# Widening the reciprocals of the softmax sums on VectorE, and the steps of a 16-group pipeline in a new order

## The reference, cut to what matters

```
x = x + attn_mlp(_layernorm(x))   # sliding window of 128, 16 heads of 16; then MLP 256 -> 1024 -> 256
x = x + rwkv_ffn(_layernorm(x))   # r = sigmoid(xr W_r); k = relu(xk W_k)^2; r * (k W_v)
x = x + mamba(_layernorm(x))      # ED 512, N 16: h = exp(delta A) h + delta B x;  y = h C + D x
x = x + expert(_layernorm(x))     # one of 8 experts for each batch, picked by the mean over its tokens
# in the attention:
scores = jnp.where(valid, scores, -jnp.inf)          # 128 queries x 256 keys for each head
attn = jax.nn.softmax(scores, axis=-1)
out = jnp.einsum('bhcqk,bhckd->bhcqd', attn, vcat)
```

## Time and profile before

| | us |
|---|---|
| median of 3 runs | 3138.97 (3136.85 to 3139.93) |
| profiled execution | 3140.19 |
| its span, first to last instruction | 3138.4 |
| mean granted TensorE clock in it | 0.946 of 2.4 GHz |
| one period of the pipeline, from 589.70 to 2591.42 us / 11 | 181.97 |

### The profile page before, as it was taken

The page is one execution under the profiler, slowest core; times in us unless marked ns, Lnnn a source line. Parts: engine busy times, 40 slices in busy tenths (PEclk is TensorE's granted clock), DMA queues, the critical chain, the costliest instruction groups (busy, mean ns, idle before and its releaser), DMA issues. The chain is left out here.

```text
span 3138.4 us, 54529 instructions
## 1 busy us (share of the span) xinstructions
PE 2770.5 (88%) x17328; PEld 1768.4 (56%) x17328; DVE 2498.8 (80%) x5626; ACT 2402.0 (77%) x5299; POOL 2657.6 (85%) x1596
## 2 busy tenths in 40 slices
PE   5888887899999999999899999989999998988667
PEld 3554454465665656566565656656565665654336
DVE  3257979888787978888787887978788897889880
ACT  6587879788787978888797887879798787865532
POOL 1108999999999999999999999999999999999880
PEclk9899999999999999999999999999999999998778
DMA  3004353446445454644546364445546455365541
GB/s 85 14 36 151 122 186 121 164 142 219 135 149 174 154 193 134 222 144 145 173 150 204 124 224 141 153 154 157 201 130 222 143 162 172 125 216 163 191 145 42
DMA packets 285965, 477.31 MB, mean 152 GB/s; under 512 B 38450, under 2 KB 93362, under 8 KB 285682
## 3 DMA queue, kind: packets, MB, share of 16 engines
q1 hardware_dynamic: 285682, 473.83, 46.0%
HBM read 388.79 MB, written 84.93 MB: 151 GB/s over the span
## 5 line engine op out<-in xcount | busy, mean ns | idle before, releaser
L1826 POOL TENSOR_TENSOR h_rows<-u_rows,b_rows 128x1024 f32<-128x1024 f32 x512 | 1201.6, 2370 | 39.3 <-PE bank L968 29.9
L1836 POOL TENSOR_TENSOR h_rows<-h_rows,c_rows 128x1024 f32<-128x1024 f32 x486 | 1145.4, 2369 | 43.6 <-DVE state L1606 30.2
L1280 ACT ACTIVATE bank<-d_rows,a_rep 128x512 f32<-128x512 f32 x1024 | 673.3, 687 | 236.6 <-DMA d_rows<-delta_dram 55.8
L1599 DVE TENSOR_TENSOR_SCAN h_rows<-bank,h_rows 128x512 f32<-128x512 f32 x492 | 586.1, 1211 | 37.0 <-ACT bank L1280 34.2
L1599 DVE TENSOR_TENSOR_SCAN h_rows<-bank,state,h_rows 128x512 f32<-128x512 f32 x480 | 590.1, 1266 | 25.9 <-ACT bank L1280 21.3
L1105 ACT ACTIVATE prob<-prob,neg_max 128x256 f32<-128x256 f32 x1024 | 508.8, 503 | 15.8 <-DVE neg_max L1377 15.6
L1377 DVE CUSTOM_DVE_ANT_0 prob<-bank,bands 128x256 f32<-128x256 f32 x896 | 335.1, 417 | 124.5 <-PE bank L803 84.9
L815 PE MATMUL bank<-ident,prob 128*128 128x128 f32 x2048 | 330.3, 286 | 59.8 <-ACT prob L1105 29.0
L815 PEld LDWEIGHTS bank<-ident,prob 128*128 128x128 f32 x2048 | 241.1, 144 | 223.1 <-issue 148.0
L968 PE MATMUL bank<-h_rows,sum_n 128*32 128x512 f32 x2048 | 297.0, 665 | 62.7 <-POOL h_rows L1836 48.3
L1036 PE MATMUL bank<-y4T,w 128*128 128x256 f32 x1024 | 248.5, 391 | 19.5 <-DMA e_b<-in_b 12.5
(11 more groups left out here) (164 smaller groups left out, 4856.1 us busy)
## 6 DMA issues: line engine op xcount, KB each, us to landing
u_rows<-u_dram SPq DMA_DIRECT2D x256, 256.0 KB, 4.1
d_rows<-delta_dram SPq DMA_DIRECT2D x256, 256.0 KB, 4.1
b_rows<-bc_dram SPq DMA_DIRECT2D x256, 256.0 KB, 3.1
c_rows<-bc_dram SPq DMA_DIRECT2D x256, 256.0 KB, 3.1
w<-in_W SPq DMA_DIRECT2D x28, 1024.0 KB, 7.0
zs_dram<-region_b SPq DMA_DIRECT2D x64, 256.0 KB, 3.3
xc_dram<-region_b SPq DMA_DIRECT2D x64, 256.0 KB, 2.8
u_dram<-region_b SPq DMA_DIRECT2D x64, 256.0 KB, 4.5
```

Of the source, the lines that this page charges most:

```text
L1280: e.activation(banks[at.bank][:, :], d_rows[:, c, :], ACT.Exp, scale=a_rep[:, k:k + 1]).then_inc(filled[at.bank], 1)
L1599: e.tensor_tensor_scan(rows, banks[at.bank][:, :], rows, start, ALU.mult, ALU.add).then_inc(drained[at.bank], 1)
L1826: e.tensor_tensor(half_of(i, b, half), u_rows[:, 2 * half:2 * half + 2, :], twice(b_rows[:, b % 2, :]), ALU.mult).then_inc(bx_ready.sem, 1)
L1836: e.tensor_tensor(rows, rows, twice(c_rows[:, b % 2, :]), ALU.mult).then_inc(hc_ready.sem, 1)
```

## The change

`widen` moves from `pool_attention` to `dve_attention`, unchanged in its text: the same copy of 128x128 with the source broadcast, the same semaphores, at the same beat (one behind `reciprocals`). On VectorE, it stands in the step after its reciprocals. `act_expert` loses both waits ahead of its first step; the wait for t5.1 is put just before the first relu, as a wait for the bank to be drained. All numbers in `PLACES`, `THREADS` and `LEADS` are new.

```diff
 PLACES = {
     "head": (
-        -1814, -1814, -921, 471, 810, 828,
+        -1272, -1272, -182, -182, 767, 767,
     ),
...
     "route": (
-        33846, 33885, 34132,
+        33266, 33977, 33977,
     ),
...
             yield from range(3)
 
         def act_expert(e, i):
-            e.wait_ge(*w1_there(i))
-            if i + 1 < 2 * BATCH:
-                e.wait_ge(*full(uses["back", i + 1, "t5.1"]))
             for half in range(2):
                 yield
                 for j in range(KM // 2):
                     at = uses["expert", i, f"e{half}.{j}"]
+                    if j == 0 and half == 0 and i + 1 < 2 * BATCH:
+                        e.wait_ge(*gone(uses["back", i + 1, "t5.1"]))
                     e.wait_ge(*full(at))
                     if j == 0 and half:
                         e.wait_ge(*full(uses["expert", i, f"e{half - 1}.5"]))
...
                     e.wait_ge(*rden_wide_ready.at(i, w - 1))
                 e.reciprocal(rden[:, heads], den[:, c % 2, heads]).then_inc(rden_ready.sem, 1)
 
+            def widen(w):
+                k = w % 2
+                e.wait_ge(*rden_ready.at(i, w + 1))
+                if w > 1:
+                    e.wait_ge(*full(use(f"a{w - 2}")))
+                e.tensor_copy(rden_wide[:, k * P:(k + 1) * P].rearrange("p (h d) -> p h d", d=HD),
+                              rden[:, 8 * k:8 * k + 8].rearrange("p (h o) -> p h o", o=1).broadcast_to([P, 8, HD])
+                              ).then_inc(rden_wide_ready.sem, 1)
+
             if i == 0:
                 e.wait_ge(s_w, 16 * len(WEIGHTS))
                 for mu in ("mu_r", "mu_k"):
...
                     masked(2 * v + at - 1)
                 if beat % 8 == 2 and beat >= 10 and beat < 72:
                     reciprocals((beat - 10) // 8)
+                if beat % 8 == 3 and beat >= 11:
+                    widen((beat - 11) // 8)
                 yield
             yield
             for n in range(GT // 2):
...
             def use(name):
                 return uses["attention", i, name]
 
-            def widen(w):
-                k = w % 2
-                e.wait_ge(*rden_ready.at(i, w + 1))
-                if w > 1:
-                    e.wait_ge(*full(use(f"a{w - 2}")))
-                e.tensor_copy(rden_wide[:, k * P:(k + 1) * P].rearrange("p (h d) -> p h d", d=HD),
-                              rden[:, 8 * k:8 * k + 8].rearrange("p (h o) -> p h o", o=1).broadcast_to([P, 8, HD])
-                              ).then_inc(rden_wide_ready.sem, 1)
-
             def divide(w):
                 c, k = divmod(w, 2)
                 e.wait_ge(*gone(use(f"a{w}")))
...
             ins.then_inc(carry_in.sem, 1)
             yield from range(ATT0 - 1)
             for beat in range(AFTER - ATT0):
-                if beat % 8 == 3 and beat >= 11:
-                    widen((beat - 11) // 8)
                 if beat % 8 == 7 and beat >= 15:
                     divide((beat - 15) // 8)
                 yield
```

More of the change, by code:

```diff
@@ L103 @@
 THREADS = (
[L104 to L110, removed]
+    (("head", "attention",), (-12844, -6895, -7146, -7117, -7096, -7120, -7120, -7137, -7122, -7132, -7133, -7148, -7134, -7165, -7156, -7182)),
+    (("mlp", "rwkv", "middle",), (-6872, -7129, -7117, -7088, -7113, -7115, -7141, -7136, -7136, -7131, -7125, -7146, -7141, -7134, -7175, -7230)),
+    (("scan",), (-7131, -7088, -7076, -7106, -7111, -7120, -7111, -7120, -7134, -7121, -7120, -7131, -7131, -7165, -7235, -7037)),
+    (("back",), (-7013, -7041, -7076, -7120, -7137, -7120, -7122, -7580, -7070, -7136, -7070, -7115, -7166, -7090, -7093, -7210)),
+    (("route",), (-2843, -6904, -9043, -7034, -8168, -7143, -6974, -7260, -7119, -7258, -9093, -7062, -7350, -7320, -3017, -7590)),
+    (("fetch",), (-7188, -8208, -7262, -8104, -6569, -6898, -8206, -7330, -8120, -7246, -7942, -7830, -7759, -8084, -7847, -2296)),
+    (("expert",), (-7079, -7148, -7106, -7118, -7113, -7121, -7189, -7146, -7134, -7186, -7170, -7233, -7231, -8037, 172, 3801)),
 )
@@ L207 @@
         "head": (
-            -86, -634, 493, 111, 91, -1212,
+            0, -282, 400, -516, 276, -887,
         ),
         "attention": (
[5 rows of a table removed]
[5 rows of a table added]
         ),
         "mlp": (
-            -31, 213, -290, 252, -122, 40, 36, -1539, 317, -41, 39, 6, -52, -52, -52, -52, -76, -66, -702, -155,
-            -114, 438, -64, 958, 29, -492, -90, -408, -189, 103,
+            183, -4, 44, 632, 89, -14, 111, -485, -356, -173, -733, 492, -530, -119, 67, 0, 415, -1294, 0, -1007,
+            -318, -1693, 0, 0, 318, 0, 0, 0, 0, 0,
         ),
         "rwkv": (
-            -49, -2000, -27, 13, 200, -467, 0, 43, 250, 50, -708, 17, 319, -100, 252, -48, 54, 5, 19, -87,
+            0, -34, 136, 383, 210, 92, -48, 1, 0, -7, -7, -7, 38, 45, 0, 56, 56, -342, 122, 198,
         ),
         "middle": (
-            -654, -223, 193, -94, 0, -11, -218, -115, 90, 0, 113, 232, 0, 0, 0, -298, 165, -124, -28, 195, 40, 417,
-            -218, 6, -21, 112, 112, 2, 304,
+            0, -1016, 165, -18, -162, -27, 0, -52, -17, -663, 34, 138, -380, 84, -1220, -67, 6, 31, 310, 264, -397,
+            531, -577, 168, -113, 417, -846, -413, 242,
         ),
         "scan": (
[8 rows of a table removed]
[7 rows of a table added]
         ),
         "back": (
-            434, -658, 146, -107, -156, -270, -220, -162, -376, -605, 144,
+            -1132, 86, -60, -60, -468, -398, -449, -34, -101, 164, 162,
         ),
         "route": (
-            -1253, -253, -119,
+            -526, -38, -417,
+        ),
+        "fetch": (
+            23,
         ),
         "expert": (
-            0, 32, -166, 0, -107, 11, 80, -259, 124, 16, -202, 33, 0, 8, -105, -20, 165, 262, 13, 264, -528, 163,
-            -103, -556, -88,
+            -244, 83, 235, -1, -113, -1, 0, 29, 190, -145, 37, -40, -1, -190, -62, -10, 224, -153, 84, 124, -9, 89,
+            127, 590, 111,
         ),
@@ L250 @@
         "head": (
-            64, 66, 237, 357, 356, 108,
+            109, 35, 730, 94, 255, 165,
         ),
         "attention": (
[5 rows of a table removed]
[5 rows of a table added]
         ),
         "mlp": (
-            -50, 124, 254, 366, 665, 1925, 584, -161, 58, 429, -184, -184, -300, -105, -92, -227, -39, 130, 130, 0,
-            323, 0, 0, 0, 0, 0, 0, 0, 0, 0,
+            233, -92, -39, -116, -137, 1863, 1464, 396, 675, 40, 58, 7, -167, 0, 0, 0, 26, 0, 0, 0, 0, 368, -476,
+            271, -1015, -121, 117, -99, -658, -879,
         ),
         "rwkv": (
-            0, 0, 0, 0, -54, 1, -213, -489, -249, -249, -241, -241, -256, -192, 427, 326, 227, 259, 295, 295,
+            0, -225, -56, -823, -552, -396, -162, -359, -411, -484, -86, 204, 173, -154, -78, -124, 249, 697, 67,
+            -12,
         ),
         "middle": (
-            276, -11, -11, -68, -68, -68, -131, -172, -172, -190, 100, 340, -28, -28, 26, 0, 0, 0, 0, 0, 0, 0, 0, 0,
-            0, 0, 0, 252, 252,
+            -109, 70, 219, 287, 219, 237, 266, 516, 337, 1237, 641, 641, 470, 926, 729, 600, 191, 166, -710, 179,
+            361, -185, -116, 410, 784, 200, -76, 256, 93,
         ),
         "scan": (
[7 rows of a table removed]
[7 rows of a table added]
         ),
         "back": (
-            241, 0, -7, -41, 394, 10, -676, -274, -964, 123, -55,
+            165, 152, -104, 208, -10, 146, -239, -228, 843, -316, 639,
         ),
         "route": (
-            -188, -237, -307,
+            -324, 479, 20,
         ),
         "fetch": (
-            -433,
+            -494,
         ),
         "expert": (
-            1025, -112, -54, 0, 0, 0, -48, -48, -237, -391, -48, -48, -48, -48, 0, 0, 0, 0, 0, 0, -90, 0, 0, 0, 0,
+            -622, -198, -118, 207, -716, 486, 0, 591, 760, 142, 585, 107, 107, -584, -156, 156, -6, 43, 43, 56, 56,
+            56, 397, 415, 251,
         ),
```

86 lines of the change are left out of this document (43 added, 43 removed), and 152 rows, old and new, of tables (LEADS, PLACES).

## The result

The changed kernel takes 3203.42 us (median of 4 runs, 3199.28 to 3207.46) against 3138.8 for before: ratio 1.0204, 95% interval [1.0189, 1.0219], slower by 64.6 us. Its profiled execution has a span of 3197.5 us. In the changed kernel, the numbers of the same source lines are 2 to 13 higher: L1672 is L1685, L1377 is L1379, L815 is L818.

What follows compares the result with a forecast made beforehand. TensorE was taken as the pace, 169.6 us busy of each 182.0 us period, GpSimd equally busy. Terms -10.2 - 5 - 5.5 + 11 = -9.7 us took the profiled 3140.2 to 3130.5, so 3129 us as median; range 3080 to 3170.

Steps and rivals of the forecast that it cites:

- the cover: VectorE's 134.8 us of idle time before its masks would absorb the 146 us of copies: +11 us, bounds 0 and +194.
- the gains: TensorE's wait for the widened tile (-10.2 us) and the two moves in the order (-5 and -5.5): 20.7 us together.
- The price of the copy: Each widening copy on VectorE takes 1.14 us, 146 us for 128; bounds 0.2 and 2.57 us each.
- C: Copies wait for GpSimd's products in each attention's first two quads, where TensorE already waits on VectorE: 3160 us, chance 0.30.
- B: GpSimd sets the pace, so losing copies and the waits before them gives -70 us, 3069 us; chance 0.08.
- The widened tile: TensorE's wait before the matmul that spreads widened reciprocals (L837) goes: -10.2 us, bounds 0 and -10.2.
- The order: Router's mean earlier on VectorE: -5 us (0 to -16.2); ScalarE's scaling for the norm behind the mlp earlier: -5.5 (0 to -11).
- ScalarE's edit: Dropping ScalarE's waits for expert weights ahead of an expert's relus gains 0, bounds 0 and -2.6 us.
- The filling and the end: In the filling nothing is late for GpSimd, and the pipeline's end holds no widening: 0 for both.

Runs made afterwards that it cites:

- e9: Changed kernel, new order kept, widening on VectorE by a one-element reduction instead of the copy: 3148.61 us, 1.0025 of before.
- e2: Kernel before, with its order and ScalarE's waits; only the widening copy moved to VectorE: 3232.48 us, 1.0299 of before.
- e10: Kernel before, in its old order, widening moved to VectorE as a one-element reduction: 3141.09 us, 1.0001 of before.
- e3: Kernel before, only ScalarE's two waits ahead of an expert's first step removed, t5.1 awaited (bank full) before the first relu: 3139.61 us, 0.9997.
- e4: Changed kernel, new order kept, widening by a second 128x128 reciprocal of the sums instead of the copy: 3169.98 us, 1.0096 of before.
- e15: Changed kernel, widening by reciprocals and reductions lasting about the copy's steady-state length in each quad: 3183.81 us, 1.0130 of before.
- e17: Changed kernel, each of 128 widenings given its own copy's length by reciprocals and reductions, eleven longest cut by up to 0.6 us: 3174.92 us, 1.0112.

## Why the prediction was wrong

It gave 3129 us (3080 to 3170) and the likeliest sign was wrong. The measured time is 74 us above: 45 of these are the cover, with 56 us where the term said 11, and 29 are the gains, which the sum put at 20.7 us and where e9, with a short widening in the same order, is 8 us slower than before. Point by point:

- **The price of the copy** was right: 1.14 us predicted, 0.94 measured, 120 us instead of 146; bounds 0.2 to 2.57, measured ones 0.20 to 2.44, the long ones ending with GpSimd. VectorE came to 161.4 us a period (163 predicted). That the mean came so near is in part luck: it hangs on where in a product the copies begin, and in the old order the same copies take 1.25 us (e2).
- **The cover is the step that failed**: "Term: 146 - 134.8 = +11 us". The idle time before the masks was taken as free for the copies. It shrank from 134.8 to 99.1 + 8.2 = 107.3 us, by 27.5 of the 120. VectorE's idle time is no store from which a later instruction draws: it lies where VectorE is ahead of TensorE, while the copies fall in front of scans for which TensorE waits. The prediction's own rows already pointed there: VectorE was 84% busy, TensorE 93%, in fixed orders that wait for each other. The runs put the term at 94 us in the old order (e2 against e10) and 56 in the new (1.0204 against e9's 1.0025), inside the bounds of 0 to +194 that the prediction named, and outside the range that it gave.
- **The rivals.** C had the right sign and the right mechanism (the copy waits for GpSimd), but the wrong place. TensorE's waits for neg_max before L815, which were to reach 40 us, are 9.9 us where they were 12.2 in the waits of before; the waits for scans grew instead. In the old order it would have been nearer: there all of TensorE's waits for neg_max are 41.6 us with the copy (e2) and 23.7 with the reduction (e10). Nor were the first two quads alone: in the steady state the copies of every quad took about 0.5 us or more in the mean, up to 1.5. B fell: GpSimd lost 38 us of copies and all its waits for them and the kernel is slower, and e10, which loses the same on GpSimd for 36 us of reductions on VectorE, is as fast as before.
- **The widened tile** (-10.2): TensorE still waits 7.7 us for it, for VectorE now, so 2.5 of the 10.2 went. In e10 the wait is gone whole, and the kernel is no faster.
- **The order** (-5 and -5.5): the wait for the mean fell from 16.2 to 1.7 us, nearly to its bound, and yet with reductions for the widening the new order is 8 us slower than the old one (e9, e10); a wait that goes is not a gain when the engine stands next for something else. For the transposes of zb, TensorE's wait for ScalarE fell by 11.5 us over the whole run (123.9 to 112.4), more than the 5.5 forecast, but its idle time before them by 2.2 only (124.7 to 122.5), for waits for x and neg_max took the place. The count of 112 widenings right behind their reciprocal was too high: in the trace it is 107, and three of the others stand behind the mean and three behind the pick. What the new order does bring was not among the terms: a microsecond of widening at constant length costs 0.2 to 0.4 us in it, 0.4 to 0.9 in the old one.
- **ScalarE's edit** (0): right as far as e3 has it.
- **The filling and the end** (0): right as far as shown: 43.0 us of the loss lie in the eleven periods, and the other 16.1 are about 3.9 for each of the groups outside them.

So of the 64 us (0.0204 x 3139), by the ratios, 8 are for the new order with a widening of 0.28 us (e9), 22 more for one of 0.95 us (e4), and 34 for its being a copy. Of these 34, 11 are for lengths that differ by quad (e15 against e4). The other 23 are for lengths that differ from group to group, or for something in the wait beyond its length; e17, which was to tell these apart, fell 19 us of VectorE short, and this stays open.

## What to carry to other kernels

Before work is moved onto an engine with idle time, ask what of its instruction runs beside the neighbours: a copy within SBUF on VectorE lasted until GpSimd's running product ended, and the same 128 values by a one-element reduction took 0.28 us and, in the old order, cost nothing. Idle time of an engine in a pipeline of fixed orders is no cover by its sum: of 134.8 us ahead of the masks, 27.5 were used, and in the old order each further microsecond cost more than the one before. A line that takes 1 us for 2 elements a partition in the trace is such a wait, and curing it gave 0.2 to 0.3%.

## What the runs showed of the hardware that was not expected

- A reciprocal costs by its elements: 195 ns for 128x8, 951 for 128x128, so (951 - 195) / 120 = 6.3 ns each, and spare ones of 40 and 72 elements took 400 and 603 ns. A narrow one with a reduction behind it that widens is the cheaper pair (0.20 + 0.28 us).
- Copies of 128x128 took 0.23 us in the filling, where GpSimd mostly stands, and up to 2.44 beside its products, always ending 80 to 90 ns behind one of GpSimd's instructions where they were longer than 0.3 us.
- The waits are locked in phase. In the old order, the first quad's copy began 0.06 us behind a product in the row shown, and the same copy lasted 2.3 to 2.4 us in every group from the fourth on. Averages over chance (half a product) don't hold in a pipeline that repeats.
